# The first batches of an attention stage set up in another order: raw weight pieces later, the first q/k split on VectorE, spills sent piece by piece, constants issued from ScalarE's queue

## What is computed

```
q, k, v = x @ wq.T, x @ wk.T, x @ wv.T            # 16 heads of 8 features
attn = softmax(q k^T / sqrt(8) - slope[h] * |i - j|)
x = layernorm(x + (attn v) @ wo.T + bo)
h = silu((x @ w1.T) * s1) * ((x @ w2.T) * s2)      # 128 -> 512, w1, w2, h1, h2, w3 are ternary times a factor
h = gelu((h @ h1.T) * s3); h = gelu((h @ h2.T) * s4)
x = layernorm(x + (h @ w3.T) * s5)                 # 512 -> 128
```

## Time and profile before

| | |
|---|---|
| median of 3 runs | 879.19 us |
| the profiled execution | 880.13 us, span 878.3 us |
| PE busy | 814.5 us, 93% of the span |
| DVE busy | 639.1 us, 73% |
| ACT busy | 621.6 us, 71% |
| POOL busy | 315.8 us, 36% |
| DMA | 81.22 MB, mean 92 GB/s |

### The profile page before, as it was taken

The page is one execution under the profiler, slowest core; times in us unless marked ns, Lnnn a source line. Parts: engine busy times, 40 slices in busy tenths (PEclk is TensorE's granted clock), DMA queues, the critical chain, the costliest instruction groups (busy, mean ns, idle before and its releaser), DMA issues. The chain is left out here.

```text
span 878.3 us, 22823 instructions
## 1 busy us (share of the span) xinstructions
PE 814.5 (93%) x8322; PEld 578.9 (66%) x8322; DVE 639.1 (73%) x1300; ACT 621.6 (71%) x1093; POOL 315.8 (36%) x491
## 2 busy tenths in 40 slices
PE   1599999999999999999999859999999999999994
PEld 1366666666666666666666537888888888888873
DVE  4578888787878787878788445677777777777774
ACT  4067777777777777777777727777777777777772
POOL 7455555555555555555564520000100000000001
PEclk9999999999999999999999969999999999999998
DMA  4775656555656555555664201011111111111001
GB/s 134 151 164 136 139 146 140 147 145 128 140 143 157 128 149 128 147 130 147 141 146 82 63 20 31 24 37 36 36 36 37 36 36 36 36 36 36 25 24 49
DMA packets 101950, 81.22 MB, mean 92 GB/s; under 512 B 11808, under 2 KB 94880, under 8 KB 101856
## 3 DMA queue, kind: packets, MB, share of 16 engines
q1 hardware_dynamic: 100976, 77.05, 35.8%
q0 software_dynamic: 880, 2.88, 1.4%
HBM read 45.82 MB, written 33.55 MB: 90 GB/s over the span
## 5 line engine op out<-in xcount | busy, mean ns | idle before, releaser
L656 DVE TENSOR_REDUCE negmax<-ps_a 128x2 f32<-128x512 f32 x512 | 327.8, 683 | 73.1 <-PE ps_a L411 69.6
L584 ACT ACTIVATE probs<-ps_b 128x512 f32<-128x512 f32 x512 | 281.1, 596 | 59.0 <-PE ps_b L411 57.6
L396 PE MATMUL ps_a<-qk_stack 52*128 52x256 bf16 x1024 | 192.6, 278 | 31.5 <-DMA qk_stack<-qk_scratch 18.2
L404 PE MATMUL ps_b<-qk_stack 54*128 54x256 bf16 x1024 | 187.0, 274 | 0.7 <-ACT probs L584 0.7
L922 ACT ACTIVATE gelu_f<-ps_r,sc 128x512 f32<-128x512 f32 x128 | 88.3, 690 | 79.8 <-PE ps_r L863 72.3
L411 PE MATMUL ps_a<-corner_sb,eye_sb 64*128 64x128 bf16 x1024 | 141.7, 220 | 0.0
L411 PE MATMUL ps_b<-corner_sb,eye_sb 64*128 64x128 bf16 x1024 | 138.6, 216 | 0.6 <-issue 0.6
L454 PE MATMUL ps_o<-probs,v_aug 128*32 128x256 f32 x2048 | 137.0, 385 | 0.0
L396 PEld LDWEIGHTS ps_a<-qk_stack 52*128 52x128 bf16 x1024 | 64.2, 95 | 101.9 <-issue 54.7
L1020 POOL TENSOR_SCALAR vareps_f<-meanvar_f 128x4 f32<-128x4 f32 x16 | 5.7, 354 | 334.9 <-DVE meanvar_f L1006 334.9
L860 PE MATMUL ps_r<-g1h,h_hi 128*128 128x512 f32 x256 | 102.8, 401 | 1.9 <-DVE g1l L987 1.9
(11 more groups left out here) (101 smaller groups left out, 1465.7 us busy)
## 6 DMA issues: line engine op xcount, KB each, us to landing
qk_stack<-qk_scratch SPq DMA_DIRECT2D x64, 384.0 KB, 5.8
qk_scratch<-qk_sb SPq DMA_DIRECT2D x64, 192.0 KB, 2.5
qk_scratch<-qk_sb SPq DMA_DIRECT2D x96, 128.0 KB, 2.5
xT_sb<-in_xT SPq DMA_DIRECT2D x32, 128.0 KB, 2.2
qk_stack<-mrow SPq DMA_DIRECT2D x256, 2.0 KB
x_sb<-in_x SPq DMA_DIRECT2D x32, 128.0 KB, 2.6
x_scratch<-x_sb SPq DMA_DIRECT2D x32, 128.0 KB, 2.0
x_in<-x_scratch SPq DMA_DIRECT2D x32, 128.0 KB, 2.1
```

The lines of the kernel that those rows point to most:

```text
L396: pe.matmul(ps_a[a_bank(k)][:, qb * SEQ:(qb + 1) * SEQ], q_stack[i][rows_of, j, qb * P:(qb + 1) * P], k_stack[i][rows_of, j, :], start=(qb ...
L404: pe.matmul(ps_b[B_BANK[k]][:, kb * SEQ:(kb + 1) * SEQ], k_stack[i][rows_of, j, kb * P:(kb + 1) * P], q_stack[i][rows_of, j, :], start=(kb ...
L584: nc.scalar.activation(probs[:, h % HALF, :], ps_b[B_BANK[k]][:], ACT.Exp, scale=slope[h]).then_inc(exp_done, 1)
L656: nc.vector.tensor_reduce(negmax[:, h_a // HALF, h_a % GROUPS, h_a % HALF // GROUPS, :], ps_a[a_bank(k)][:].rearrange("p (b k) -> p b k", ...
```

## The change

Four things are moved.

1. **Pieces.** The 11 raw weight pieces are split in steps 2 to 12 instead of -4 to 1 and 27 to 31. The load of a piece is issued one step ahead of its split (steps 1 to 11).
2. **Start of ACT and DVE.** ACT copies q and k of batches 0, 1 and 2 before it lays the rows of that step (in slot 12, behind the copy), instead of laying rows 0 first. DVE makes the four split instructions of batch 0 (`split_first`), directly behind the scaling of `wq`, and lays all rows and constants behind that. POOL's `split_qk` begins with batch 1 and waits for `qk_split` of the batch before.
3. **Spills.** `spill` waits for each part by itself: one DMA behind `qk_first`, two behind `qk_second`, two behind `qk_split`. The last two are 192 KB (three parts of q) and 128 KB.
4. **Constants.** `wq`, `qscale`, `eye`, `corner` and `ident` are issued by ACT, ahead of its first instruction, at the same time as SP issues x, `wk` and the rows. `wv`, `wo` and `bo` are issued by SP behind the stack of batch 0, with a semaphore of their own (`late_landed`).

```diff
-        const_landed = sem("const_landed")
+        const_landed, late_landed = sem("const_landed"), sem("late_landed")
...
-        piece_at = [*range(FIRST, 2), *range(BATCH - 5, BATCH)]
-        assert len(pieces) == N_PIECES == len(piece_at)
+        PIECE_FIRST = 2
+        piece_at = range(PIECE_FIRST, PIECE_FIRST + N_PIECES)
+        assert len(pieces) == N_PIECES
...
-        N_CONST, N_QK_CONST = 6, 3
+        N_CONST, N_QK_CONST, N_LATE = 3, 3, 3
...
-            for dst, src in ((wq_sb, wqT), (qscale_sb, qscale), (wk_sb, wkT)):
-                sp.dma_start(dst[:], src).then_inc(qk_const_landed, DMA)
+            sp.dma_start(wk_sb[:], wkT).then_inc(qk_const_landed, DMA)
             sp.dma_start(rows_sb, rows).then_inc(rows_landed, DMA)
-            for dst, src in ((eye_f, eye), (corner_f, corner), (id_sb, ident), (wv_sb, wvT), (wo_sb, woT), (bo_sb, bo)):
-                sp.dma_start(dst[:], src).then_inc(const_landed, DMA)
-
-            def spill(par):
+
+            def spill(b, par):
                 parts, terms = qk_sb[par], qk_dram[par].rearrange("n r d h t -> n (d h) r t")
-                for first, last in ((0, 3), (3, 5)):
-                    sp.dma_start(terms[0, :, first:last, :], parts[:, 0:last - first, 0, :]).then_inc(spilled, DMA)
-                for first, last, r in ((0, 3, 0), (3, 5, 1)):
-                    sp.dma_start(terms[1, :, first:last, :],
-                                 parts[:, r, 1, :].unsqueeze(1).broadcast_to([P, last - first, SEQ])).then_inc(spilled, DMA)
+                wait(sp, qk_first, b + 1)
+                sp.dma_start(terms[1, :, 0:3, :],
+                             parts[:, 0, 1, :].unsqueeze(1).broadcast_to([P, 3, SEQ])).then_inc(spilled, DMA)
+                wait(sp, qk_second, b + 1)
+                sp.dma_start(terms[1, :, 3:5, :],
+                             parts[:, 1, 1, :].unsqueeze(1).broadcast_to([P, 2, SEQ])).then_inc(spilled, DMA)
+                sp.dma_start(terms[0, :, 3:5, :], parts[:, 0:2, 0, :]).then_inc(spilled, DMA)
+                wait(sp, qk_split, b + 1)
+                sp.dma_start(terms[0, :, 0:3, :], parts[:, 0:3, 0, :]).then_inc(spilled, DMA)
                 sp.dma_start(terms[:, :, 5, :].rearrange("n p t -> p n t"),
                              parts.rearrange("p r n t -> p (r n) t")[:, 0:6:5, :]).then_inc(spilled, DMA)
...
-                    wait(sp, qk_split, t + 4)
                     wait(sp, stacked, (t + 3) * GROUPS * DMA)
-                    spill(1 - par)
+                    spill(t + 3, 1 - par)
...
             for t in range(FIRST, LAST + 1):
                 step(t, t % STACKS)
+                if t == FIRST + 1:
+                    for dst, src in ((wv_sb, wvT), (wo_sb, woT), (bo_sb, bo)):
+                        sp.dma_start(dst[:], src).then_inc(late_landed, DMA)
...
+                if t == 0:
+                    pe.wait_ge(late_landed, N_LATE * DMA)
...
-                    if (t, k) in ((FIRST, 15), (FIRST + 1, 0), (FIRST + 1, 15)):
-                        lay_rows({(FIRST, 15): 1, (FIRST + 1, 0): 2, (FIRST + 1, 15): 3}[t, k])
-
-            act.wait_ge(rows_landed, DMA)
-            lay_rows(0)
+                    if t < FIRST + 3 and k == 12:
+                        act.wait_ge(rows_landed, DMA)
+                        lay_rows(t - FIRST)
+                        if t == FIRST + 2:
+                            lay_rows(3)
+
+            for dst, src in ((wq_sb, wqT), (qscale_sb, qscale)):
+                act.dma_start(dst[:], src).then_inc(qk_const_landed, DMA)
+            for dst, src in ((eye_f, eye), (corner_f, corner), (id_sb, ident)):
+                act.dma_start(dst[:], src).then_inc(const_landed, DMA)
...
+            def split_first():
+
+                parts = qk_sb[0]
+                dve.wait_ge(qk_copied, 1)
+                nc.vector.tensor_copy(parts[:, 0, :, :], qk_f[:]).then_inc(qk_first, 1)
+                dve.wait_ge(qk_first, 1)
+                nc.vector.tensor_tensor(qk_rest[:], qk_f[:], parts[:, 0, :, :], ALU.subtract).then_inc(qk_left, 1)
+                dve.wait_ge(qk_left, 1)
+                nc.vector.tensor_copy(parts[:, 1, :, :], qk_rest[:]).then_inc(qk_second, 1)
+                dve.wait_ge(qk_second, 1)
+                nc.vector.tensor_tensor(parts[:, 2, :, :], qk_rest[:], parts[:, 1, :, :], ALU.subtract).then_inc(qk_split, 1)
...
-                        n = piece_at.index(t - 1)
+                        n = t - 1 - PIECE_FIRST
...
-                    if t == FIRST and k == 15:
-                        lay_rows(1)
-                    if t == FIRST + 1 and k == 0:
-                        lay_constants()
-                        lay_rows(2)
-                    if t == FIRST + 1 and k == 15:
-                        lay_rows(3)
             dve.wait_ge(qk_const_landed, N_QK_CONST * DMA)
             nc.vector.tensor_tensor(wqs_sb[:], wq_sb[:], qscale_sb[:], ALU.mult).then_inc(wq_scaled, 1)
+            split_first()
             dve.wait_ge(rows_landed, DMA)
             lay_rows(0)
+            lay_constants()
+            for i in range(1, STACKS):
+                lay_rows(i)
...
                 wait(pool, qk_copied, b + 1)
+                wait(pool, qk_split, b)
                 wait(pool, spilled, (b - 1) * SPILLS * DMA)
                 nc.gpsimd.tensor_copy(parts[:, 0, :, :], qk_f[:]).then_inc(qk_first, 1)
...
-                if t in piece_at:
-                    load_piece(piece_at.index(t))
+                if t + 1 in piece_at:
+                    load_piece(t + 1 - PIECE_FIRST)
                 if live(t, BATCH):
                     split_max(t, 1)
-                if live(t + 3, BATCH):
+                if live(t + 3, BATCH) and t + 3 > 0:
                     split_qk(t + 3, qk_sb[1 - par])
...
-                        pool.wait_ge(const_landed, N_CONST * DMA)
+                        pool.wait_ge(late_landed, N_LATE * DMA)
...
-                    split_piece(piece_at.index(t))
+                    split_piece(t - PIECE_FIRST)
```

## The result

The changed kernel took a median of 868.96 us (four runs, 867.9 to 870.36) beside 879.62 us for the kernel before on the same chip: a ratio of 0.9879, with a 95% interval of 0.9861 to 0.9897, so some 10.7 us faster. The forecast was 867.7. The profiled execution took 867.9, with a span of 866.1, against the 880.13 and 878.3 of the one before.

What follows compares the result with a forecast made beforehand. The prediction took the lead-in chain to PE's first score, then 32 fixed-pace steps, as the bound. Gains of 10.5 (first score) and 1.0 (end) made 11.5: 880.13 to 868.6 profiled, 867.7 us as median, range 865.0 to 872.0.

Steps and rivals of the forecast that it cites:

- Constants: Lead-in: `wk` is issued 0.94 earlier by SP, so DVE's scaling starts at 3.28 instead of 4.22.
- the first rival: Lead-in: ACT pays 1.25 for each DMA issue, making batch 0's copy 2.5 later; 870.2 us, chance 0.08.
- Copy and split: Lead-in, batch 0: copy starts at 5.8, gaining 2.95; split on DVE takes 2.5, ending at 8.9, gain 7.7 by then.
- Spill and stack: Lead-in: last spill DMA at 9.4, landing 2.5, stack issued at 11.9, 7.4 to first score at 19.3, gain 10.5.
- The 1.3 that I allowed for lighter company of the stack: Batch 0's stack: up to 1.3 more gained if the lighter transfers beside it count in bytes; not in the forecast.
- The rival in which the round trip keeps its 3.66: Lead-in: spill's landing keeps 3.66 and DVE's layings cost 1, losing 2.2; 869.9 us, chance 0.08.
- Behind the first score: From first score onward: nothing else holds PE, batch 1's slack of 0.87 stays, and the whole 10.5 is carried.
- The pace: Full steps: pieces in steps 2 to 12 and SP's three spill waits cost zero; steps stay at 14.39.
- open looks: Full steps with pieces: 11 looks at 0.68 are not hidden, giving back 7.5; 875.2 us, chance 0.03.
- SP's queue: Full steps: three spill waits delay the rows of maxima, losing 12 us; 880 us or over, chance 0.04.
- nothing moves: Lead-in still ends at 47 because something else binds, and only the end's 1.0 stays; 878.2 us, chance 0.03.
- The end: Steps 28 to 30 lose their look: 0.5 gained each in 28 and 29, 1.0 in all, between 0 and 1.4.

Runs made afterwards that it cites:

- SP's old order: The changed kernel, but SP issues all constants in its old order, ahead of the second x: 870.77 us, ratio 0.9892.
- the kernel with the old pieces: The changed kernel with the raw pieces back at steps -4 to 1 and 27 to 31, each load in its split's step: 872.26 us, ratio 0.9904.
- the kernel with the split alone: The kernel before with only batch 0's split moved to DVE, ahead of its layings, POOL starting at batch 1: 874.37 us, ratio 0.993.
- SP's order: The changed kernel, but a spill waits for the stack of two batches before, and a stack for the one before: 868.49 us, ratio 0.9868.
- the version by halves: The changed kernel with SP's order, batch 0's stack in four DMAs, PE starting after two, DVE laying rows 3 later: 865.42 us, ratio 0.9829.
- DVE quiet: The changed kernel with batch 0's split on POOL and DVE waiting for it before laying anything: 870.16 us, ratio 0.9893.
- the split on POOL: The changed kernel, but POOL splits batch 0 as before, beside DVE's laying of rows: 872.56 us, ratio 0.9916.

## Why the prediction was right, step by step

**The forecast** of 867.7 stood 1.3 below the measured median, inside its range; the main term, the first score at 19.3, was measured at 19.39. Under that sum single terms were off in both directions.

**Constants, the term mis-sized most.** Forecast was the scaling at 3.28, it came at 3.79: 0.43 instead of 0.94. I took the 2.09 from issue to landing as fixed, and it was 2.60. ACT's `qscale` was issued at 1.18, just ahead of `wk` at 1.19, and the scaling waits for both; that company slows the transfers is not shown. The ten profiles with ACT's issues have 2.41 to 2.62, but the four in which SP issues all constants scatter from 2.02 and 2.09 to 2.46 (the kernel before with the pieces moved) and 2.59 (with the split on DVE), so the 2.09 that I built on may have been a low one. My sentence that no row shows two engines issuing at once overlooked one in the trace of before: POOL issued a raw piece at 2.25, while SP was issuing `wk` (2.13 to 2.56).

```profile
2.25 0.78 POOL L714 DMA_DIRECT2D raw<-in_w1T  x1
```

That ACT pays no more than SP for an issue is shown by its five (0.42 to 0.46), and with that the first rival fell.

**Copy and split** followed, half a microsecond late: the copy at 6.31 (5.8), the split in 2.33 where I had 2.5 with the handovers, ended at 9.27 (8.9). POOL and DVE taking turns, which I noted in passing, was the larger part of this edit's worth: 2.28 of 3.50.

**Spill and stack** gave nearly all of it back. The last spill DMA went out at 10.04 (9.4), 0.77 behind the split's end where I had 0.5, but the landing took 2.14 (2.5) and the way back 7.21 (7.4). That the terms' errors cancel to 0.1 at the first score is luck; that the sum of them is near is not. The 1.3 that I allowed for lighter company of the stack has no working: with three constants beside it the way back took 7.21, with none (SP's old order) 7.20. My reason, that no raw piece travels beside the spill, is what the kernel with the old pieces shows (3.13). The rival in which the round trip keeps its 3.66 fell with it. I had put the pieces' worth at the landing alone; the kernel before with only the pieces moved gained 4.83 at the first score: the rows landed by 5.40 instead of 6.95, so that the copy came at 7.21 and not at 8.77, and POOL came to q and k at once. Whether the piece had held the rows up isn't shown: in the kernel with the split alone, which has the pieces, they were there by 6.44.

**Behind the first score** all of it was carried in the first profile, as I said, after a dip to 9.81 at step 0; in the second some 0.9 of it was not, by PE's pace, which my sum has no term for. The wait of the earlier trace rows shrank from 0.94 to 0.37:

```profile
37.33 0.37 PE L400 MATMUL ps_a<-qk_stack 52*128 52x256 bf16 x1 [0.37 <-DMA qk_stack<-mrow]
```

**The pace.** With 11 pieces in steps 2 to 12 the copies of q and k are 14.38 apart, also around a look, as in the earlier trace rows:

```profile
104.75 0.68 DVE L702 TENSOR_REDUCE lo_max<-w_lo 128x1 f32<-128x512 f32 x1
...
104.94 0.60 ACT L615 ACTIVATE qk_f<-ps_m 128x512 f32<-128x512 f32 x1 [0.28 <-PE ps_m L519]
...
119.32 0.60 ACT L615 ACTIVATE qk_f<-ps_m 128x512 f32<-128x512 f32 x1 [0.28 <-PE ps_m L519]
```

The looks are hidden, and SP's three waits were met in full steps: the rivals of open looks and of SP's queue fell. That nothing moves fell with the first score.

**The end** gave 0.74, not 1.0. I had doubled the 0.26 of the earlier trace rows; the steps with a look were 0.37 longer each.

**The sum** by these terms is 10.38 + 0.74 = 11.1, and the medians differ by 10.7; the ratio's interval, 9.1 to 12.2 us of 879.62, holds both. The two profiles of the changed kernel stand 12.1 and 10.3 ahead of the one of before at the last `v_aug`, so a microsecond either way was not the forecast's to hit. The high end of my range, 872.0, is not reached by what I named for it: 870.2 with the end's 1.0 gone is 871.2.

## What to carry to other kernels

Read the lead-in of a pipelined kernel as one chain, up to the first instruction of the engine that bounds the rest, and price each link from steady steps where nothing is beside it: where a link is longer at the start than later, what stands beside it is the thing to move. Work for a later stage belongs in full steps where the engines that it uses wait anyway, not in the lead-in. When the chain is short, cut its longest transfer so that the consumer can begin on a part of it; with SP's order it gave 4.3 us here (2.8 at the first score), where the order alone gave about one, within the noise.

## What the runs showed of the hardware beside that

**POOL and DVE took turns**, in both directions and for the whole instruction. With DVE quiet POOL's cast of 128x512 took 0.61 and its subtraction 1.15; beside DVE's casts 1.10 to 1.49 and 1.41 to 2.01. DVE's cast of 0.43 took 1.37 and its subtraction of 0.69 took 1.00 beside POOL's splitting of a piece. The stretch is no slower working but the rest of the other engine's instruction, so it depends on where that one stands.

**PE's pace behind the first score.** The same four matmuls of v took 0.71 before, 1.22 after and 0.71 in the version by halves, while the granted clock of each profile reads 1.00 there. The windows of before at the start of its step 0, and of after at the same place (start:end, length, busy us and instructions of PE, PEld, DVE, ACT, POOL, then clock, DMA share, GB/s):

```profile
29.77:49.15 19.38, 16.82 (x104) 10.47 (x106) 14.36 (x23) 2.33 (x5) 9.05 (x14) 1.00 0.67 158
...
49.40:52.80 3.40, 3.40 (x49) 2.63 (x44) 3.08 (x5) 3.04 (x6) 1.41 (x2) 0.51 1.07 157
```

```profile
19.39:39.34 19.95, 17.99 (x104) 11.13 (x106) 13.20 (x21) 5.93 (x8) 7.24 (x11) 1.00 0.62 148
```

From the first score to the copy of `v_aug` PE did the same 104 matmuls in 16.82 us of busy time before and 17.99 after. In before a single score matmul fell from 0.42 to 0.27 at 46.5, went back to 0.42 from 49.4 to 52.2 (there the clock does read 0.51) and then stayed at 0.27; in after it stayed at 0.42 until 40.5, and was 0.27 from then on. In this pair that is the dip of 0.57 at batch 0, and the 0.46 that came back in step 0.

The 1.00 of the column is no reading there: the first clock entry that the traces hold stands at 45.9 in before, 40.6 in after and 32.7 in the version by halves, and up to it the column shows full clock for want of an entry. The durations say otherwise. 0.42 is what this matmul takes where the clock reads 0.51, the lower of its two levels (1.2 GHz), and it took 0.42 up to about that entry, after PE had been idle for 7.46 us and more ahead of its first score. So PE ran its first scores at the lower level in each of these three kernels. When the clock rises differs between executions of one kernel: in the second profile of the changed kernel the first entry is at 43.8. Step 0 there is the same 190 matmuls in 13.26 us of busy time, not in 12.16:

```profile
39.34:51.84 12.50, 12.16 (x190) 8.12 (x190) 9.79 (x16) 9.77 (x21) 3.60 (x7) 1.00 0.78 173
```

```profile
39.41:52.81 13.40, 13.26 (x190) 8.88 (x190) 9.94 (x16) 10.20 (x21) 3.50 (x7) 1.00 0.74 168
```

What sets the moment was not tried.

**Pauses of single steps.** In most profiles one or a few of the 32 steps is longer by 0.3 to 1.5 us, each time another one: in place of 14.39 it is 14.74 (from 392.81) in before, 15.00 (153.77) with SP's constants, 15.83 (141.45) with the split on POOL, 15.28 (395.83) with SP's order. The one whose rows are shown above, at 468.82, has no releaser in the trace; what causes them stays open. They and the moment of PE's rise are of the size by which executions of one kernel differ, so that an edit of 0.7 us is seen in the first score of a profile and not in the times.
